# Two row transposes moved to the head of their step, two groups of feature matmuls to the tail of the next

## The reference

```
x = x + attn(layernorm(x))                 # 16 heads of 16, softmax features
x = x + xattn(layernorm(x), ctx)           # 8 heads of 32, 77 keys each
x = x + ffn(layernorm(x))                  # causal attention, 8 heads of 64, 8 gated experts
```

```
q = xn @ Wq + bq                           # per row of x
weight = softmax(q k^T / sqrt(32))         # 77 keys per head: 616 columns per row
x = x + (weight v) @ Wo + bo
```

## Time and profile before

| | |
|---|---|
| Runs, us | 974.97, 979.66, 980.01 |
| Profiled execution, us | 980.92 |
| Its span from first to last instruction, us | 979.1 |
| Mean granted tensor clock | 0.994 |
| Busy: PE, DVE, ACT, POOL | 938.1, 682.1, 390.3, 236.5 us |
| Steps 9 to 14 of the first batch | about 104 to 132 us |
| The same of the second batch | about 584 to 612 us |

### The profile page before, as it was taken

One profiled execution on the slowest core, in us unless ns is written; L12 is line 12 of the kernel. 1 busy time (PEld: TensorE's weight loads), 2 busy tenths in 40 slices (PEclk: granted clock), 3 DMA queues, 4 the chain that ended last, 5 costly groups with the idle time before them and its releaser, 6 DMA issues.

```text
span 979.1 us, 14699 instructions
## 1 busy us (share of the span) xinstructions
PE 938.1 (96%) x5620; PEld 730.3 (75%) x5620; DVE 682.1 (70%) x1054; ACT 390.3 (40%) x680; POOL 236.5 (24%) x253
## 2 busy tenths in 40 slices
PE   6889999999999999999999998999999999999998
PEld 3668778887756655789976785888876656659998
DVE  3767566547557867988868475765574777879887
ACT  3644555130466766401023355630205655761000
POOL 6212412222533312136610032300032101411000
PEclk9999999999999999999999899999999999999999
DMA  8003000433245511255630000023121000022753
GB/s 257 26 25 127 1 1 1 148 117 129 65 150 185 182 63 45 60 172 178 179 123 1 1 1 2 1 60 119 46 88 39 23 22 0 22 76 84 206 178 125
DMA packets 33739, 81.56 MB, mean 83 GB/s; under 512 B 5847, under 2 KB 10551, under 8 KB 33671
## 3 DMA queue, kind: packets, MB, share of 16 engines
q1 hardware_dynamic: 32391, 76.44, 24.8%
q10 hardware_dynamic: 1280, 4.20, 1.6%
HBM read 61.26 MB, written 19.20 MB: 82 GB/s over the span
## 4 chain that ended last, share of the span: by engine, by line
PE 79%; DVE 10%; ACT 4%; DMA 3%; issue 3%; POOL 1%; ACTq 0%; SPq 0%; DVEq 0%; POOLq 0%
PE ps L1097 18%; PE ps L1403 10%; PE ps L1340 8%; PE ps L1255 5%; PE ps L1409 5%; PE ps L1300 5%; PE ps L1105 4%; PE ps L1316 3%; PE ps L1207 3%; PE ps L1269 3%; DVE region L989 3%; PE ps L1222 2%; PE ps L1376 2%; PE ps L1377 2%; PE ps L1239 1%
## 5 line engine op out<-in xcount | busy, mean ns | idle before, releaser
L1340 PE MATMUL ps<-region 128*128 128x512 f32 (+3 forms) x384 | 161.4, 503 | 0.0
L968 DVE TENSOR_REDUCE region<-ps 128x1 f32<-128x512 f32 (+1 forms) x192 | 98.2, 551 | 64.1 <-PE ps L1319 64.1
L749 ACT ACTIVATE region<-ps 128x512 f32<-128x512 f32 x192 | 92.2, 486 | 122.7 <-PE ps L1379 110.7
L1013 DVE COPY_PREDICATED region<-region,ps 128x512 f32<-128x512 uint32 x112 | 82.0, 736 | 72.0 <-PE ps L1097 71.4
L1403 PE MATMUL ps<-expert_hi,kst 128*128 128x256 f32 x512 | 125.1, 282 | 4.1 <-DVE kst L1043 2.2
L1403 PE MATMUL ps<-expert_lo,kst 128*128 128x256 f32 x512 | 123.3, 279 | 0.0
L1097 PE MATMUL ps<-expert_hi,wide_hi 128*128 128x512 f32 x256 | 102.7, 401 | 0.0
L548 ACT ACTIVATE region<-ps 64x512 f32<-64x512 f32 (+4 forms) x146 | 80.8, 556 | 50.2 <-PE ps L1222 23.1
L1097 PE MATMUL ps<-expert_hi,wide_lo 128*128 128x512 f32 x256 | 100.2, 391 | 0.0
L1403 PEld LDWEIGHTS ps<-expert_hi,kst 128*128 128x128 f32 x512 | 96.0, 187 | 5.3 <-DVE kst L1043 2.6
L1097 PE MATMUL ps<-expert_lo,wide_hi 128*128 128x512 f32 x256 | 99.8, 390 | 0.0
(11 more groups left out here) (148 smaller groups left out, 1782.7 us busy)
## 6 DMA issues: line engine op xcount, KB each, us to landing
region<-hot_rows SPq DMA_DIRECT2D x128, 128.0 KB, 3.4
expert_hi<-halves_kept SPq DMA_DIRECT2D x24, 512.0 KB, 3.7
expert_lo<-halves_kept SPq DMA_DIRECT2D x24, 512.0 KB, 5.0
halves_kept<-expert_hi SPq DMA_DIRECT2D x16, 512.0 KB, 5.2
halves_kept<-expert_lo SPq DMA_DIRECT2D x16, 512.0 KB, 5.9
expert<-in_value_experts SPq DMA_DIRECT2D x8, 512.0 KB, 4.2
expert<-in_output_experts SPq DMA_DIRECT2D x8, 512.0 KB, 4.3
gb<-gate_rows ACTq DMA_DIRECT2D x16, 256.0 KB, 3.9
```

The costliest lines, as they stand in the source:

```text
L749: act.activation(PT[:, g % RING, lo:CH], ps[:, 4 + g % 2, 0:CH - lo], ACT.Exp).then_inc(sem["pt_ready"], 1)
L968: dve.tensor_reduce(mx[:, i, at_mx:at_mx + 1], ps[:, max_bank(h, m), 0:w], AX.X, ALU.max).then_inc(sem["s_max"], 1)
L1013: dve.copy_predicated(V3_heads[:, t], chosen.unsqueeze(3).broadcast_to([P, PAIRS3, 2, HD3]), ps[:, n % 4, :].rearrange("p (a i k) -> p a i ...
L1340: mm(ps[:, SUM_BANK[c], lo:CH], V3[:, j, h // 2, h % 2 * HD3:(h % 2 + 2) * HD3], PT[:, g % RING, lo:CH], start=(j == 0), stop=(j == TC * ( ...
```

## The change

In steps 9 and 13 (PROJECTED) the row transposes of tile 3 and tile 7 are issued at the head of the step on the tensor engine (behind the features where the step has any), and their copy to xT at the head of the step on the scalar engine. The query projection stays at the end. In steps 10 and 14 (LATE) the cross attention's features are issued behind the output projection on the tensor engine, the maxima and the subtraction behind the X add and the statistics on the vector engine, and the exponential behind the row copy on the scalar engine. The number of instructions and DMAs is the same.

```diff
+        PROJECTED = tuple(c * TC + TC + 5 for c in range(NC))
+        LATE = tuple(s + 1 for s in PROJECTED)
 # scalar
+                    if s in PROJECTED:
+                        norm_evac(b, 1, s - 6)
                     for a, t in due(s, 1):
                         until(act, "fT_ps", b, a * TT + t + 1)
...
                     for a, t in due(s, 0):
-                        if s != 1:
+                        if s != 1 and s not in LATE:
                             features_exp(a, t)
...
                     for a, t in due(s, 6):
-                        norm_evac(b, a + 1, t)
+                        if s not in PROJECTED or a:
+                            norm_evac(b, a + 1, t)
...
+                    if s in LATE:
+                        for a, t in due(s, 0):
+                            features_exp(a, t)
 # vector: the maxima and subtraction of a step become features(s)
+                    if s not in LATE:
+                        features(s)
...
                         step(dve.tensor_tensor(X[:, b, t, :], ps[:, 5, 0:D], X[:, b, t, :], ALU.add))
                         norm_stats(b, a + 1, t)
+                    if s in LATE:
+                        features(s)
 # tensor: the feature matmuls of a step become features(s)
+                    if s not in LATE:
+                        features(s)
+                    if s in PROJECTED:
+                        norm_transpose(b, 1, s - 6)
...
+                    if s in LATE:
+                        features(s)
                     for a, t in due(s, 6):
-                        norm_transpose(b, a + 1, t)
+                        if s not in PROJECTED or a:
+                            norm_transpose(b, a + 1, t)
```

More of the change, by code:

```diff
@@ L892, in place_sums, with features @@
                                         ).then_inc(sem["n_blk"], 1)
-                for s in range(LAST):
-                    if s - 2 in GATES_AT:
-                        gates(GATES_AT.index(s - 2))
+                def features(s):
                     for a, t in due(s, 0):
@@ L917, in _ @@
                         last.then_inc(sem["f_sub"], 1)
+                for s in range(LAST):
+                    if s - 2 in GATES_AT:
+                        gates(GATES_AT.index(s - 2))
+                    if s not in LATE:
+                        features(s)
                     if s == 2:
```

## The result

Nine runs of the changed kernel have a median of 982.97 us (981.83 to 989.61), nine of the kernel before 978.96 (974.97 to 980.77). The ratio is 1.0047 with a 95% interval of 1.0032 to 1.0063: slower, clear of noise, with its middle inside the half per cent that the prediction calls no change. The forecast was 983.0. The profiled execution after took 981.83 us, with a span of 980.0.

The account below looks back on a forecast made before the run. The tensor engine, busy 96% of the span, was taken as the bound. Losses of 0.68 and 1.01 make 1.7 a batch, 3.4 in two; on the 979.66 median that gives 983, likeliest range 980.7 to 984.7, full range 976 to 988.

Parts of the forecast that it names:

- Head of step 9: Tile 3's row transposes wait 0.63 for tile 2's copy out of bank 7, replacing 0.64 at the projection; gain 0.0.
- Head of step 13: Tile 7's row transposes wait 0.59 for tile 6's copy, replacing 0.99 at the projection; gain 0.40.
- Tail of step 10: Bias hidden, but DVE delivers late; features of step 11 start at 115.74 against 115.06, a loss of 0.68.
- Tail of step 14: Bias hidden, but a PE wait of 2.2 replaces 0.78; loss 1.01 with step 13's gain included.
- What is late next: DVE, with X add and statistics ahead of the maxima: 1.07 + 1.02 + 1.78 from output projection to next features.
- rival 2: A wash: DVE delivers maxima earlier at steps 11 and 15, up to 1.02 each; -0.7, 979.0; 0.12 together with Rival 3.
- rival 4: Tensor clock drops in the new gaps behind steps 10 and 14, 3.4 a drop, up to 989.9; chance 0.16.
- A clock under 1.00 in the window behind 133: Listed sign that the forecast is wrong: tensor clock below full behind the new gap at 131.1 to 133.3.
- Rival 1: The stalls at the four boundaries go and nothing takes their place: -6.4, 973.3; chance 0.08.
- Rival 3: The change doesn't do what it says: projection, and for completeness also features, still wait; 0.12 together with rival 2.
- The rule on banks: Two bank 7 groups brought together give the sum its two stalls; without the rule, no stalls and a loss of 1.0.

Follow-up runs that it names:

- e1: Changed kernel with only the heads of steps 9 and 13 changed, late features put back, against the kernel before: 978.51 us against 978.86, ratio 0.9998.
- e3: Changed kernel with maxima and subtraction ahead of X add and statistics on the vector engine, against the kernel before: 981.52 us against 978.86, ratio 1.0029.
- e5: Changed kernel plus four unread matmuls filling the tensor engine's gap in step 14, against the kernel before: 985.78 us against 979.13, ratio 1.0060.
- e2: Changed kernel with only the late features of steps 10 and 14, row transposes and copy put back, against the kernel before: 984.29 us against 978.86, ratio 1.0058.
- e4: Row transposes behind covering matmuls, features behind one group only, DVE and exponentials as before, against the kernel before: 975.36 us against 978.86, ratio 0.9962.
- e5b: e5 run once more beside other kernels, against the kernel before: 985.17 us against 979.06, ratio 1.0056.
- e7: e5 with three more unread matmuls in step 2, against the kernel before: 980.79 us against 979.06, ratio 1.0019.
- e6: e4 with three unread matmuls in step 2, against the kernel before: 975.03 us against 979.06, ratio 0.9961.

## Why the prediction was right, and where it wasn't

**Head of step 9.** Forecast: a stall of 0.63 for one of 0.64. Measured: from the transposes' slot end at 105.31 to 106.03, 0.72; the projection 0.1 later. Confirmed by e1. The release of 0.05 taken from bias and features was too short for one of transposes: by the timeline of ACT, the copy of tile 2 ends at 105.51 + 0.38 = 105.89, and PE's next transposes start 0.14 later.

```profile
105.51 0.38 ACT L551 ACTIVATE xT<-ps 128x256 f32<-128x256 f32 x1 [0.21 <-PE ps L1094]
```

**Head of step 13.** Forecast: a stall of 0.59, gain 0.40. Measured: 0.70 (123.36 - 122.66), gain 0.27.

**Tail of step 10.** Forecast: + 0.68 with the head. Measured: + 0.39 and + 0.11. **Tail of step 14.** Forecast + 1.41 without the head's gain, measured + 1.05. In both the step that was off is the end of the projection: I let the next work start 3.70 after it, which is the length of the row; from start to start it costs 3.44 (109.13 to 112.56). The tails were 0.30 and 0.36 cheaper than forecast, 0.26 of each for this reason, the heads 0.12 and 0.13 dearer: 0.4 a batch, which takes the 3.4 to 2.5.

**Mechanism.** What is late next was named right, and the chain from the output projection through X add, statistics, maxima and subtraction to the next features, put at 3.87, took 3.84 (112.78 to 116.62). What DVE's order is worth was put too high, in rival 2: of the 1.02 that the X add and the statistics take ahead of the maxima, e3 gives 0.26 back. The prediction said that the feature matmuls, done at 113.63, are not what the maxima wait for (113.96); their difference, 0.33, is the price, and it could have been read off there.

**The clock.** It was rival 4, with 0.16. It is not another case but a part of the result: 1.6 us behind each longer gap in the profile, and 1.9 us by the mean clock of the change run again. A clock under 1.00 in the window behind 133 is among the signs that the prediction itself named as showing it wrong, and it is there, 0.91. That the forecast's 983 is hit is luck in part: the waits were put 0.9 too high, the clock at nothing, and the median of before at 979.66, which is 978.96 over nine runs. The loss was forecast as 3.4 and measured as 4.0, 2.5 of it waits. Rival 4's 3.4 a drop was twice too dear, since the low clock lasted 3.6 us there and not 6.8 as at the place of the earlier trace rows. The Trainium skill (TensorE: Matmul & The Clock Gate, section What's actually happening) says that the throttled clock is the default and that activity releases it. At this place the traces of e5 agree, 1.00 with the gap filled for 0.91 with it empty; but the second batch of e2 kept 1.00 behind the same empty gap.

**Rivals 1 to 3.** Rival 1 (-6.4) fell: the stalls moved. But e4 shows that 4.4 of its 6.4 were there to be had in another order. Rival 2 needed the 1.02 back, and e3 bounds it at 0.26. Rival 3 fell: neither the projection nor the late features wait; at step 9 the stall went to the row transposes, as said.

**The rule on banks.** The two stalls at bank 7 are in the trace (0.56 and 0.62). The Trainium skill (Perfetto Trace Analysis, section Matmuls) advises to rotate over banks, which speaks against this order; e4 shows both stalls gone with matmuls between two users of one bank. Another bank wasn't tried.

## What to carry to other kernels

Work put ahead of a waiting instruction should be just long enough to fill the wait; each group beyond that delays the chain that the instruction starts, and the wait comes back one step later, where nothing is left to cover it. Before an operation is pulled forward, look at who used its buffer last: right behind the previous user it only changes one stall for another. And take the cost of a matmul group from start to start, not from its row's length. Before two profiled spans are compared, set their low clock and their waits for transfers against each other: here a transfer hid 1.6 of 2.5 us.

## What was not expected of the hardware

A gap of 2.08 us on PE was followed by half clock in both batches of two profiles of the change, by half clock in one batch and full clock in the other in e2, and one of 1.83 by full clock in e3. Filled (e5, e5b, e7), the same place kept full clock in six batches of six. Behind the gap of 1.7 in step 10 the clock fell in one batch of twelve, the first of e7. Behind the two shorter gaps of step 2 (0.97 and 0.79) it fell in 17 batches of 20, and in none of four with them filled, so the length of a gap alone doesn't decide. Filling one place kept the clock up at that place, yet did not lower the time of the whole in e5; only with step 2 filled too (e7) did it fall. Where the clock falls differs between profiles of kernels that are the same up to that point (20 to 40 us in e5 and e6, full clock there in the change), so a single profile can't price it. The mean over the runs did so within 0.7 us for six kernels of ten, and was 1.5 to 2.3 off for the others.
